# Two DMA sends of a windowed-attention kernel change queue and place in the opening

## The reference

```python
y = layernorm(x, g1, b1)                       # shifted by (-2, -2), cut into windows of 128 tokens
q, k, v = split(windows(y) @ qkv_w + qkv_b)    # per head, q scaled by 8 ** -0.5
attn = softmax(q @ k.T + bias[None] + mask)    # bias per head, mask per window
x = x + unwindow(attn @ v @ proj_w + proj_b)
z = layernorm(x, g2, b2)
return x + gelu(z @ fc1_w + fc1_b) @ fc2_w + fc2_b
```

## Time and profile before

| | |
|---|---|
| median of three runs | 223.86 us |
| profiled execution | 224.5 us, of which the span is 222.7 us |
| TensorE busy (matmuls) | 202.6 us, 91% of the span |
| VectorE, ScalarE, GpSimd busy | 164.7, 149.6 and 128.2 us |
| granted TensorE clock, mean | 0.992 of full speed |

### The profile page before, as it was taken

How to read it: one execution, slowest core, us unless ns; L and a number is a source line. 1 busy time by engine, 2 the same in 40 slices (tenths; PEclk the granted TensorE clock), 3 DMA queues, 4 the chain that set the end, 5 groups by cost and what they waited for, 6 DMA issues and landing times.

```text
span 222.7 us, 10176 instructions
## 1 busy us (share of the span) xinstructions
PE 202.6 (91%) x4376; PEld 123.5 (55%) x4376; DVE 164.7 (74%) x253; ACT 149.6 (67%) x217; POOL 128.2 (58%) x116
## 2 busy tenths in 40 slices
PE   0889775999999999999999999999999999979884
PEld 0854532576576667656765666566557666453221
DVE  3896863676797788878797877787766867857874
ACT  7465366566867678768867776767546654677883
POOL 7775589353339874895689398623642092240840
PEclk9999999799999999999999999999999999999999
DMA  6816427565425542553355134414540000000333
GB/s 202 252 57 171 138 98 203 157 191 176 145 61 169 181 135 68 158 169 106 100 166 149 37 122 122 153 52 132 179 130 4 6 6 7 1 3 0 125 113 141
DMA packets 24292, 25.54 MB, mean 115 GB/s; under 512 B 3556, under 2 KB 21732, under 8 KB 24164
## 3 DMA queue, kind: packets, MB, share of 16 engines
q1 hardware_dynamic: 23496, 24.16, 34.6%
q10 hardware_dynamic: 752, 0.74, 1.2%
HBM read 16.24 MB, written 8.39 MB: 111 GB/s over the span
## 4 chain that ended last, share of the span: by engine, by line
POOL 39%; issue 38%; PE 11%; ACT 4%; DVE 4%; DMA 2%; POOLq 1%; DVEq 0%; ACTq 0%
POOL rstd L376 17%; POOL X L406 5%; POOL parts L394 4%; POOL yn L386 3%; POOL xc L368 3%; POOL X L411 3%; PE ps L966 3%; DMA X<-x_tok 2%; ACT q_rows L740 2%; POOL mean L356 1%; ACT k_rows L740 1%; POOL var L362 1%; PE pq L966 1%; PE pav L996 1%; PE ps L1018 1%
## 5 line engine op out<-in xcount | busy, mean ns | idle before, releaser
L524 DVE TENSOR_REDUCE negm<-ps 128x8 f32<-128x1024 f32 x64 | 78.1, 1223 | 26.3 <-PE ps L900 25.8
L735 ACT ACTIVATE prob<-ps 128x1024 f32<-128x1024 f32 x64 | 65.5, 1023 | 24.2 <-PE ps L929 21.7
L376 POOL TENSOR_TENSOR rstd<-var,neghalf 128x16 f32<-128x16 f32 x16 | 47.4, 2963 | 16.0 <-DVE var L489 15.1
L914 PE MATMUL ps<-rel_j,id_b 96*32 96x512 bf16 x512 | 40.0, 384 | 3.6 <-ACT prob L735 2.4
L949 PE MATMUL pav<-prob,va 128*32 128x128 f32 x1024 | 41.6, 281 | 0.0
L949 PEld LDWEIGHTS pav<-prob,va 128*32 128x32 f32 x1024 | 24.3, 110 | 12.6 <-issue 6.0
L929 PE MATMUL ps<-q_rows,k_rows 64*64 64x128 bf16 x1024 | 27.0, 223 | 1.3 <-DMA q_rows<-m_mid 1.3
L929 PEld LDWEIGHTS ps<-q_rows,k_rows 64*64 64x64 bf16 x1024 | 16.5, 107 | 19.9 <-issue 14.4
L900 PEld LDWEIGHTS ps<-k_rows,q_rows 64*64 64x64 bf16 x1024 | 22.3, 108 | 6.6 <-issue 0.4
L900 PE MATMUL ps<-k_rows,q_rows 64*64 64x128 bf16 x1024 | 25.5, 218 | 0.0
L876 PE MATMUL ps<-rel_i,ident_b 64*64 64x512 bf16 x256 | 25.1, 382 | 0.0
(11 more groups left out here) (134 smaller groups left out, 336.1 us busy)
## 6 DMA issues: line engine op xcount, KB each, us to landing
slots<-parts SPq DMA_DIRECT2D x21, 256.0 KB, 2.5
q_rows<-slots SPq DMA_DIRECT2D x42, 128.0 KB
k_rows<-slots SPq DMA_DIRECT2D x40, 128.0 KB
X<-x_tok SPq DMA_DIRECT2D x8, 256.0 KB, 4.2
y_tok<-res SPq DMA_DIRECT2D x7, 256.0 KB, 2.0
q_rows<-m_hi SPq DMA_DIRECT2D x32, 4.0 KB
q_rows<-m_mid SPq DMA_DIRECT2D x32, 4.0 KB
bias_parts<-rel_parts SPq DMA_DIRECT2D x3, 128.0 KB
```

Source lines behind the costliest of these rows:

```text
L376: pool.tensor_tensor(rstd[:, i, :], var[:, i, :], neghalf[:], ALU.pow).then_inc(rstd_done[i], 1)
L524: dve.tensor_reduce(dst, first_home(j)[:].rearrange("p (a u n) -> p a u n", u=2, n=TOK), AX.X, ALU.max, negate=True).then_inc(max_done, 1)
L735: act.activation(prob[:, j % NPROB, :], ps2[:], ACT.Exp).then_inc(exp_done, 1)
L914: pe.matmul(ps2[32 * c:32 * (c + 1), 512 * e:512 * (e + 1)], id3_b[0:96, :], rel_j[0:96, c, e].unsqueeze(2).to_broadcast([96, 2, 2, TOK]), ...
```

## The change

In the sync engine's block the gather of image 1's high q leaves the step `p = -2` and stands in the step `p = 0`, behind `send_max(1)`, which opens that step. The gather of image 1's middle k leaves ScalarE's block and stands in the sync engine's, between that of the middle q and that of the low q.

```diff
                 if p == -2:
                     scatter(1, HIGH)
                     scatter(1, MID)
+                if p == 0:
                     gather(sp, 1, HIGH, 0)
-                if p == 0:
                     scatter(1, LOW)
                     gather(sp, 1, HIGH, 1)
                     gather(sp, 1, MID, 0)
+                    gather(sp, 1, MID, 1)
                     gather(sp, 1, LOW, 0)
                     gather(sp, 1, LOW, 1)
...
                 if 0 <= p < PAIRS:
                     exponential(p)
-                if p == 0:
-                    gather(act, 1, MID, 1)
                 if p >= 0 and n < B and s in (1, 3):
                     middle_part(n, s // 2)
```

## The result

| | changed kernel | kernel before |
|---|---|---|
| four executions of each | 227.61 us median (225.97 to 228.36) | 223.94 us median (223.63 to 228.16) |
| ratio, first comparison | 1.0158, 95% interval 1.0087 to 1.023 | |
| ratio, second comparison (12 and 35 executions) | 1.0083, 1.0042 to 1.0123; median 227.69 us | 225.71 us median |
| profiled execution | 225.97 us, span 224.2 us | 224.5 us, span 222.7 us |

The ratios leave out executions more than 1.5% above the fastest of their kernel (in the second comparison 14 of the 35 of the kernel before and 1 of the 12 of the changed one), while the medians in us are of all executions. The change made the kernel slower, by 0.8 to 1.6%; both intervals lie above 1. The medians are 3.7 us apart in the first comparison, of four executions each, and 2.0 us in the second.

The account below looks back on a forecast made before the run. TensorE was taken as the limit from 45 us on. Queue 0.1 plus low clock 1.4 made 1.5 us: 226.0 profiled, 225.4 against the median, taken as 225.2 since low clock may partly lie inside the hole; range 223.3 to 226.1.

Parts of the forecast that it names:

- ScalarE, and the early send: In the opening, exponential(1) starts 1.8 us earlier; send_max(1) is issued by 32.2, removing TensorE's 0.28 us wait before scores_s2(2).
- The sync engine's queue: Ahead of send_max(2), 1.16 us of issues leave and 1.25 come: scores_s2(4) 0.1 us later, at 43.8 (43.5 to 45.0).
- The hole: Ahead of scores_s2(4), TensorE has nothing to do from 40.3 to 43.8, about 3.5 us.
- The clock, once: Behind the wait before scores_s2(4), TensorE runs at the low clock for 3.4 us, costing 1.4 us.
- The clock's bound: Low clock behind the wait before scores_s2(4) costs between 0, if absent or inside the wait, and 1.7 us.
- Rival C: Sync engine's queue still later: scores_s2(4) starts 0.7 to 1.2 us later, plus the low clock, 226.1 to 226.6 us; chance 0.09.
- the time behind the opening: From 45 us on TensorE is the limit; only its entry into that stretch or its clock counts, so nothing was added.
- The step from the profile to the median: Whole kernel: the median lies 0.6 us below the profiled execution of 224.5 us, so 226.0 becomes 225.4.
- The direction: Whole kernel gets slower: 1.9 us gained in the opening is spent waiting before scores_s2(4), low clock comes behind; 225.2 us.

Follow-up runs that it names:

- e1: The kernel before with only send_max(1) moved ahead of image 1's first gather, the middle k gather staying on ScalarE; ratio 0.9995 to the kernel before.
- e2: The kernel before with only image 1's middle k gather moved from ScalarE to the sync engine; ratio 1.0105 to the kernel before, median 227.69 us.
- e5: The changed kernel with image 1's middle k gather back on ScalarE, behind exponential(2); ratio 1.0037 to the kernel before, median 226.68 us.
- e7: The changed kernel with send_max(2) ahead of the middle and low gathers, all twelve gathers on the sync engine; ratio 1.0176 to the kernel before.
- e12: The changed kernel again, unchanged, a second further look at one execution with its granted clock; 229.49 us.
- e11: The changed kernel again, unchanged, one further look at an execution with its granted clock; 229.36 us.
- e3: The changed kernel with 11 dummy matmuls on TensorE right ahead of scores_s2(4); ratio 1.005 to the kernel before, median 226.59 us.
- e9: As e5, with 9 dummy matmuls on TensorE ahead of scores_s2(4); ratio 1.0045 to the kernel before, median 225.62 us.
- e10: As e5, plus send_max(2) ahead of the middle and low gathers and 9 dummy matmuls ahead of scores_s1(8); ratio 1.0053 to the kernel before.

## Why the prediction was wrong

Point by point, by its own steps:

- **ScalarE, and the early send: right.** 1.8 us forecast for `exponential(1)` and 1.8 found, counted from `exponential(0)`; the send by 32.2 forecast, at 31.71 and 32.27 found, and the wait ahead of `scores_s2(2)` gone.
- **The sync engine's queue: right in kind, short in size.** 0.1 us forecast for `scores_s2(4)`, 0.63 found in the first profile. The moved pair cost 1.3 us (e1 against the changed kernel), as the 1.25 costed; what the send's leaving frees was 0.67 us in e1 (8.49 to 7.82 us) and not the 1.16 of the sum, because other issues took longer. The term is also no sharper than the queue: `scores_s2(4)` started at 43.75 and 44.05 in two profiles of the kernel before, and at 44.38, 44.29, 43.78 and 45.14 in four of the changed one, the last outside my bounds (43.5 to 45.0). e2 and e5 show that these two issues hold the send, and e7 that the last gather would hold TensorE nearly as long without it.
- **The hole: right.** 3.5 us forecast, 3.65, 3.83, 3.50 and 4.35 us found in four profiles.
- **The clock, once: right.** 1.4 us forecast, 1.33 found. The sum for the profiled execution was 226.0 us, and it took 225.97, but that is partly luck: the opening put it 1.96 us behind and not 1.5, and the kernel before gave 0.46 us back by a longer step at `scores_s2(42)`, which is in no term of the sum.
- **The clock's bound: this step failed.** I wrote that its bounds were "0, if it does not fall or falls inside the hole, and 1.7, half of 3.4". The stretch of low clock behind a hole is not always 3.4 us: in e12 and e2 it was some 6.8, and it cost 2.75 us in e12. One more can come behind another wait (e11). 10 of the changed kernel's 18 executions had a mean clock of 0.988 or below, as these have (0.985), so the median is near them. Rival C, which should have reached there, priced a later queue and not a longer low clock.
- **A term put at nothing: the time behind the opening.** I wrote that from 45 us on the opening "counts only if it changes when TensorE enters that full stretch, or its clock in it", and added nothing for the rest. The rest is not fixed: between `scores_s2(9)` and the last, relative to the first profile of the kernel before, its second profile lost 1.7 us, and the changed kernel's four lost -0.5, 1.5, 3.3 and 0.9 us, by waits for maxima behind long issues and by the low clock behind one of them. That spread is larger than the effect. Whether the change makes such waits more frequent is not shown.
- **The step from the profile to the median: failed too.** I took 0.6 us off because three executions had a median of 223.86. Over 82 executions the kernel before has 225.6 us, above its profiled 224.5. With the sum's 1.5 us on that, the time would have been 227.1; the changed kernel's 18 have 227.9. In the first comparison, where the kernel before again had 223.94, this step was not the fault: there the difference of 3.7 us between four executions each is larger than the 2.0 to 2.3 of the longer counts.
- **The direction** came from the right mechanism: the gain is spent waiting, and the low clock comes where it is not hidden. The profiles show the clock's part, 1.33 and 2.75 us, and e3 that dummy work prevents it; the times of e3, e9 and e10 only point the same way.

What stays open is why e3, e9 and e10, with the clock high, still have ratios of about 1.005, although their medians are within 0.9 us of the kernel before's, and why the same ten issues on the sync engine take 7.3 us in one execution and 9.8 in another.

## What to carry to other kernels

When a wait is taken out of an early chain, look for the next in-order queue that all of it must pass, and count issues there as work: 0.6 us each on a queue with no pause is as real as a matmul. A gain ahead of a fixed arrival becomes idle time, and all ten of TensorE's waits of 2.3 to 4.4 us that these profiles show from 40 us on had low clock behind them. A range for a kernel whose clock falls in only some of its executions needs the longest stretch of low clock, the spread of the waits further on, and a base of more than three executions.

## What the runs showed of the hardware

- Behind a wait of TensorE the granted clock was at the lower level, 1.2 GHz, for some 3.4 us in some executions and 6.8 us in others, with the same work ahead. In the changed kernel it was 3.4 us behind holes of 3.50, 3.65 and 3.83 us and 6.8 behind one of 4.35; in e2 it was 6.8 us behind 3.41, and in e9 behind 2.34. (The lengths are estimates from the clock of the stages.)
- The kernel before, too, ran at a mean clock from 0.977 to 1.0, and its times sort by it: 224.8 us at 0.997 and above, 228.1 us at 0.980 to 0.988. One execution had 0.662 and took 282.24 us.
- The same ten gathers of 128 KB took 7.3 to 9.8 us to issue from the sync engine ahead of `scores_s2(50)`, in different profiles. Three of them together took from 1.83 to 3.54 us. The 4 KB send behind them was late for TensorE by 0.3 to 2.7 us, and was itself used 1.6 to 2.0 us behind its issue.
